# First attention with its rows of values in six visits per group, its lead-in and the middle stage's end reordered

## The reference

```python
x = L0_attn_x                              # (4, 1024, 128), float32
x = _layernorm(x + _L0_attn_ref(x, ...))   # 16 heads of 8
x = _layernorm(x + _L0_ffn_ref(x, ...))    # 8 experts, top 1, hidden 512
x = _layernorm(x + _L1_attn_ref(x, ...))   # 16 heads of 64
x = _layernorm(x + _L1_ffn_ref(x, ...))    # gated, hidden 512
```

```python
Q = proj(Wq, bq); K = proj(Wk, bk); V = proj(Wv, bv)
scores = einsum('bhid,bhjd->bhij', Q, K) / sqrt(hd)
decay = where(causal, 0.0, -abs(delta) ** ALPHA)      # delta = i - j, causal: delta < 0
scores = where(causal, -inf, scores) + decay
attn = softmax(scores, axis=-1)
return einsum('bhij,bhjd->bhid', attn, V) ... @ Wo.T + bo
```

## Time and profile before

| | us |
|---|---|
| three runs | 2277.38, 2282.85, 2283.62 |
| median | 2282.85 |
| the profiled execution | 2285.02 |
| its span, first to last instruction | 2283.2 |
| mean granted clock of PE | 0.951 |

### The profile page before, as it was taken

How to read it: one execution, slowest core, us unless ns; L and a number is a source line. 1 busy time by engine, 2 the same in 40 slices (tenths; PEclk the granted TensorE clock), 3 DMA queues, 4 the chain that set the end, 5 groups by cost and what they waited for, 6 DMA issues and landing times.

```text
span 2283.2 us, 34398 instructions
## 1 busy us (share of the span) xinstructions
PE 2072.3 (91%) x11728; PEld 1169.3 (51%) x11728; DVE 1513.8 (66%) x3409; ACT 1210.0 (53%) x1923; POOL 779.2 (34%) x480
## 2 busy tenths in 40 slices
PE   5899999998487999877999999999999999999998
PEld 2333333334476555544555555555555555655644
DVE  3877777774732778865888878888887875333311
ACT  2366666667343678853656555555565553223232
POOL 5000000000601111003777777777777773000000
PEclk7899999999588999986999999999999999999999
DMA  5233333111265579656666666666666667543300
GB/s 177 95 125 128 120 120 127 57 51 62 98 186 145 172 231 293 200 169 141 170 166 170 165 152 152 150 159 169 163 169 152 164 158 209 135 103 84 88 5 9
DMA packets 230189, 319.11 MB, mean 140 GB/s; under 512 B 22316, under 2 KB 152668, under 8 KB 229608
## 3 DMA queue, kind: packets, MB, share of 16 engines
q1 hardware_dynamic: 214712, 289.04, 46.2%
q0 software_dynamic: 7664, 24.39, 3.0%
q10 hardware_dynamic: 7640, 3.48, 0.5%
HBM read 176.91 MB, written 105.84 MB: 124 GB/s over the span
## 4 chain that ended last, share of the span: by engine, by line
PE 28%; DVE 16%; issue 8%; SPq 1%; DMA 1%; ACT 0%; DVEq 0%
PE ps L1252 10%; DVE a1mx L968 4%; PE ps L916 4%; DVE a1KB L982 3%; DVE a1mx L972 3%; PE ps L900 3%; DVE a1QB L982 3%; PE ps L870 2%; PE ps L901 2%; PE ps L1203 2%; DVE a1mx L965 2%; PE ps L1263 1%; PE ps L1240 1%; PE ps L1241 1%; DVE ps L965 1%
## 5 line engine op out<-in xcount | busy, mean ns | idle before, releaser
L1088 POOL TENSOR_TENSOR a1sum<-a1sum,a1prob 128x1024 f32<-128x1024 f32 (+3 forms) x256 | 489.0, 1910 | 64.9 <-ACT a1prob L1025 33.5
L1025 ACT ACTIVATE a1prob<-ps 128x512 f32<-128x512 f32 (+2 forms) x640 | 326.0, 562 | 252.7 <-PE ps L903 238.4
L468 DVE TENSOR_REDUCE a0grid<-ps 128x8 f32<-128x1024 f32 x288 | 346.7, 1221 | 118.9 <-PE ps L344 64.9
L569 ACT ACTIVATE a0prob<-ps 128x1024 f32<-128x1024 f32 x288 | 292.9, 1025 | 170.2 <-PE ps L370 91.3
L965 DVE CUSTOM_DVE_ANT_0 ps<-ps,c_mask_ij 128x128 f32<-128x128 f32 x496 | 262.7, 551 | 97.2 <-issue 95.5
L900 PE MATMUL ps<-a1QA,a1KA 69*128 69x512 f32 (+3 forms) x768 | 285.7, 379 | 5.8 <-PEq L33 3.4
L916 PE MATMUL ps<-a1prob,a1V 128*64 128x512 f32 (+3 forms) x1536 | 277.9, 505 | 0.0
L870 PE MATMUL ps<-a1KA,a1QA 68*128 68x128 f32 x744 | 241.7, 391 | 28.7 <-DVE a1mx L968 16.4
L901 PE MATMUL ps<-a1QB,a1KB 128*128 128x512 f32 (+3 forms) x768 | 264.4, 352 | 0.0
L916 PEld LDWEIGHTS ps<-a1prob,a1V 128*64 128x64 f32 x1536 | 104.4, 140 | 171.1 <-issue 144.2
L1085 POOL TENSOR_TENSOR a1sum<-a1prob 128x768 f32<-128x768 f32 x64 | 156.8, 2450 | 82.0 <-ACT a1prob L1025 79.9
(11 more groups left out here) (268 smaller groups left out, 3227.5 us busy)
## 6 DMA issues: line engine op xcount, KB each, us to landing
a1FK<-s_k SPq DMA_DIRECT2D x128, 256.0 KB, 5.3
a1FQ<-s_q SPq DMA_DIRECT2D x128, 256.0 KB, 5.8
s_xs<-c_zero POOLq DMA_DIRECT2D x19, 1024.0 KB, 9.0
s_q<-mqkT SPq DMA_DIRECT2D x32, 512.0 KB, 3.0
s_k<-mqkT SPq DMA_DIRECT2D x32, 512.0 KB, 3.0
s_v<-mv SPq DMA_DIRECT2D x32, 512.0 KB, 3.9
a1V<-s_v SPq DMA_DIRECT2D x32, 512.0 KB, 4.4
a1KA<-a1KB SPq DMA_DIRECT2D x64, 256.0 KB
```

What stands on the lines that cost most here:

```text
L468: dve.tensor_reduce(grid[g % 2][:, :, a:b + 1:b - a], banks(("max", k)), axis=AX.X, op=ALU.max).then_inc(s1_free, 1)
L569: act.activation(prob[:, :, a:b + 1:b - a, :], banks(("exp", q)), ACT.Exp).then_inc(p_full, 1)
L1025: act.activation(weights_of(g, u)[:, group[0]:group[-1] + 1, off:BANK], both(e, u, group), ACT.Exp).then_inc(weighed, 1)
L1088: pool.tensor_tensor(t[:, :, off:BANK], t[:, :, off:BANK], weights_of(g, u)[:, :, off:BANK], ALU.add).then_inc(summed, 1)
```

## The change

1. `after` gives the rows in six visits: rows 9, 10, 11 of the group before at unit 2, then 0 and 1 at 6, 2 and 3 at 8, 4 and 5 at 11, 6 and 7 at 14, 8 at 17.
2. Lead-in: three sets of high and low buffers; 13 products ahead instead of 17; PE waits only for drains in banks that the ring uses; SP stores chunk 2 before the loads of K and BQ of group 0, and chunk 4 before the first loads of group 1; ACT issues BK of group 0 after 8 products.
3. End of the middle stage: 12 maxima, the last gate jobs, 12 maxima, turn; ACT splits pair 1 there, and then sends the row of pair 0. `QB1`, `KB1` move into the buffers of the first pair (16 KB more), and the small tiles of the routing move before the assertion on its end.
4. Second attention: SP issues the copies of pair 1 ahead of its slopes and V; DVE lowers pair 1 at units 0 to 3 of group 0; ACT's splits of pair 2 stand behind units 0, 3, 4, 5, as in the other groups.

```diff
@@ -69,8 +69,7 @@
-    after = {1: ((9,), ()), 2: ((10,), ()), 3: ((11,), ()), 5: ((), (0,)), 6: ((), (1,)), 7: ((), (2,)), 8: ((), (3,)),
-             10: ((), (4,)), 11: ((), (5,)), 13: ((), (6,)), 15: ((), (7,)), 17: ((), (8,))}
+    after = {2: ((9, 10, 11), ()), 6: ((), (0, 1)), 8: ((), (2, 3)), 11: ((), (4, 5)), 14: ((), (6, 7)), 17: ((), (8,))}
...
@@ -93,7 +92,7 @@
-    EARLY, NPROD, COL = 17, len(products), dim + 1
+    PARTS3, EARLY, NPROD, COL = 3, 13, len(products), dim + 1
...
@@ -133,7 +132,7 @@
         product, xT_full, high_full, low_full, v_full = sem("product"), sem("xT_full"), sem("high_full"), sem("low_full"), sem("v_full")
-        stored = [sem("stored0"), sem("stored1")]
+        stored = [sem(f"stored{r}") for r in range(PARTS3)]
...
@@ -147,13 +146,21 @@
+        def batch_stored(engine, b):
+
+            for c in range(b * seq // CHUNK, (b + 1) * seq // CHUNK):
+                engine.wait_ge(stored[c % PARTS3], 16 * 4 * (c // PARTS3 + 1))
+
+            batch_stored(engine, g // per)
+            if g > 0:
+                batch_stored(engine, g // per)
...
@@ -171,9 +178,6 @@
-            if h == 0:
-                for r in range(2):
-                    engine.wait_ge(stored[r], 16 * 4 * (b + 1))
...
@@ -190,7 +194,7 @@
-                    nc.sync.dma_start(scr[name][r, :, c * CHUNK:(c + 1) * CHUNK], part[c % 2][:, n, :].bitcast(F32)).then_inc(stored[c % 2], 16)
+                    nc.sync.dma_start(scr[name][r, :, c * CHUNK:(c + 1) * CHUNK], part[c % PARTS3][:, n, :].bitcast(F32)).then_inc(stored[c % PARTS3], 16)
...
@@ -202,12 +206,14 @@
             store(1)
+            batch_stored(sp, 0)
             still(sp, Q[0], "q0", 0, loaded1[0])
-            sp.wait_ge(cleared, 1)
-            load_second(sp, 0)
             for c in range(2, chunks):
                 store(c)
-                if c == 3:
+                if c == 2:
+                    sp.wait_ge(cleared, 1)
+                    load_second(sp, 0)
+                if c == 4:
                     sp.wait_ge(cleared, 2)
...
@@ -418,8 +424,9 @@
                 project(n)
-            for n in range(8, EARLY - 3):
-                drained(n)
+            for n in range(8, EARLY - 1):
+                if n % 8 < 2 * RING:
+                    drained(n)
             pe.wait_ge(const["c_cast"], 4)
...
@@ -508,7 +515,7 @@
                     dve.wait_ge(high_full, 2 * c + i + 1)
-                    dve.scalar_tensor_tensor(low[c % 2][:, i, :], product_bank(n), (bq, bk)[i][:, 0:1], high[c % 2][:, i, :].bitcast(F32),
+                    dve.scalar_tensor_tensor(low[c % PARTS3][:, i, :], product_bank(n), (bq, bk)[i][:, 0:1], high[c % PARTS3][:, i, :].bitcast(F32),
                                              ALU.add, ALU.subtract).then_inc(low_full, 1)
...
@@ -561,8 +568,8 @@
-                    for r in range(2):
-                        act.wait_ge(stored[r], 16 * 4 * chunks // 2)
+                    for r in range(PARTS3):
+                        act.wait_ge(stored[r], 16 * 4 * len(range(r, chunks, PARTS3)))
...
@@ -587,9 +594,9 @@
-                if c > 1:
-                    act.wait_ge(stored[c % 2], 16 * 4 * (c // 2))
-                act.activation(high[c % 2][:, i, :], product_bank(n), ACT.Identity, bias=(bq, bk)[i][:, 0:1]).then_inc(high_full, 1)
+                if c >= PARTS3:
+                    act.wait_ge(stored[c % PARTS3], 16 * 4 * (c // PARTS3))
+                act.activation(high[c % PARTS3][:, i, :], product_bank(n), ACT.Identity, bias=(bq, bk)[i][:, 0:1]).then_inc(high_full, 1)
...
@@ -602,11 +609,12 @@
             cast_constants()
-            for n in range(6, EARLY - 1):
+            for n in range(6, 8):
                 drain(n)
             act.wait_ge(cleared_first, 1)
+            batch_stored(act, 0)
             moving(act, BK[0], "k0", 0, loaded1[0])
-            for n in range(EARLY - 1, NPROD):
+            for n in range(8, NPROD):
                 drain(n)
...
@@ -725,8 +734,8 @@
-        QA, KA, QB, KB = ([first] + [own(f"{n}{b}", [P, 2, S], F32R) for b in range(1, NB)]
-                          for first, n in ((pair0.QA, "QA"), (pair0.KA, "KA"), (pair0.QB, "QB"), (pair0.KB, "KB")))
+        QA, KA = ([first] + [own(f"{n}{b}", [P, 2, S], F32R) for b in range(1, NB)] for first, n in ((pair0.QA, "QA"), (pair0.KA, "KA")))
+        QB, KB = ([first, second, own(f"{n}2", [P, 2, S], F32R)] for first, second, n in ((pair0.QB, pair0.QB1, "QB"), (pair0.KB, pair0.KB1, "KB")))
         FQ, FK = pair0.FQ, pair0.FK
...
@@ -816,9 +825,9 @@
-            load_e(1)
+            load_e(1)
...
@@ -984,8 +993,8 @@
                 for u in range(NU):
-                    if g == 0 and 2 <= u < 6:
-                        lower(1, u - 2)
+                    if g == 0 and u < 4:
+                        lower(1, u)
                     at_units = (2, 6, 10, 11) if g > 0 else (6, 7, 10, 11)
...
@@ -1049,12 +1058,8 @@
                     exponentials(g, u)
-                    if g == 0 and u < 2:
-                        split(1, 2 * u)
-                        split(1, 2 * u + 1)
-                    at_units = (0, 3, 4, 5) if g > 0 else (4, 5, 6, 7)
-                    if g + 2 < G and u in at_units:
-                        split(g + 2, at_units.index(u))
+                    if g + 2 < G and u in (0, 3, 4, 5):
+                        split(g + 2, (0, 3, 4, 5).index(u))
                     if u == TILES - 1:
...
@@ -1964,9 +1969,9 @@
                 here.append((("xT", "gate")[n % 12 // 11], n // 12 + 1, 0))
-            if n == LAST:
-                here += [("max", k, 0) for k in range(NM)] + [("turn", 0, 0)]
+            here += [("max", k, 0) for k in range(NM // 2)] if n == LAST else []
             here += [("aug", c, 0) for c in turn_gates.get(n, ())]
+            here += [("max", k, 0) for k in range(NM // 2, NM)] + [("turn", 0, 0)] if n == LAST else []
             after_item[n] = here
...
@@ -2237,10 +2242,11 @@
-            def first_maxima():
+            def first_maxima(some):
                 mx, mx2 = pair0.mx, pair0.mx2
-                for k, (head, t, j0, j1) in enumerate(max_rows):
+                for k in some:
+                    head, t, j0, j1 = max_rows[k]
                     w, bank = j1 - j0, ps[:, 6 + at["max", k, 0] % 2, :]
...
@@ -2249,6 +2255,9 @@
                         dve.tensor_reduce(mx2[:, 0, head, t - IT // 2:t - IT // 2 + 1], bank[:, 0:w], axis=AX.X, op=ALU.max).then_inc(pair0.max_done, 1)
+            def first_row():
+
+                mx, mx2 = pair0.mx, pair0.mx2
                 dve.wait_ge(pair0.max_done, NM)
...
@@ -2274,10 +2283,12 @@
                 if n == LAST:
-                    first_maxima()
+                    first_maxima(range(NM // 2))
                 for late in (2, 3):
                         gates_b(event_of[EVENTS[n - late][0]])
+            first_maxima(range(NM // 2, NM))
+            first_row()
...
@@ -2381,11 +2392,15 @@
                     split(split_at.index(n))
-                if n == LAST:
-                    act.wait_ge(pair0.max_done, NM + 1)
-                    act.dma_start(pair0.QA[ROW:ROW + 1, :, :].bitcast(F32), pair0.neg[:, 0, :].bitcast(F32)).then_inc(pair0.row_in, 16)
                 for c in turn_gates.get(n, ()):
                     keep_aug(c)
+            act.wait_ge(pair0.loaded_f[1], 16 * 8)
+            for k in range(4):
+                which, head = k % 2, k // 2
+                buf, wide = ((pair0.FK[1], pair0.KB1), (pair0.FQ[1], pair0.QB1))[which]
+                act.activation(wide[:, head, :], buf[:, head, :], ACT.Copy).then_inc(pair0.rounded, 1)
+            act.wait_ge(pair0.max_done, NM + 1)
+            act.dma_start(pair0.QA[ROW:ROW + 1, :, :].bitcast(F32), pair0.neg[:, 0, :].bitcast(F32)).then_inc(pair0.row_in, 16)
```

More of the change, by code:

```diff
@@ L118, in attention0 @@
         xT = [over(f"xT{r}", [P, CHUNK]) for r in range(2)]
-        high, low = ([over(f"{n}{r}", [P, 2, CHUNK], F32R) for r in range(2)] for n in ("high", "low"))
+        high, low = ([over(f"{n}{r}", [P, 2, CHUNK], F32R) for r in range(PARTS3)] for n in ("high", "low"))
         rest = {n: over(n, [P, w * seq]) for n, w in (("a0q", 1), ("a0k", 1), ("a0bq", PAIR), ("a0bk", PAIR))}
@@ L645, in __init__ @@
         self.neg, self.spare = own("neg", [2 * IT, 2, P], F32R), own("spare", [P, 3])
+        self.QB1, self.KB1 = own("QB1", [P, 2, S], F32R), own("KB1", [P, 2, S], F32R)
         sem = lambda n: nc.alloc_semaphore(f"a1_{n}")
@@ L1429, in middle @@
         ye = [own(f"ye{r}", [P, P]) for r in range(RB)]
+        sort = own("sort", [P, 32 + experts * experts + 2 * NT])
+        more, ntile, tri = own("more", [P, experts, 32]), own("ntile", [P, experts]), own("tri", [P, experts, experts])
+        cum, ended, te, st = own("cum", [P, experts]), own("ended", [P, NT, experts]), own("te", [P, NT]), own("startt", [P, NT])
+        started, rowf = own("started", [P, NT, experts]), own("rowf", [P, NT])
+        info = own("info", [P, 2, NT], I32)
```

(5 more changed lines are left out.)

## The result

The changed kernel takes 2294.35 us (median of five runs, 2293.52 to 2300.74) against 2282.85: 1.0064 of the kernel before by the means of the runs, 95% interval 1.0049 to 1.0080, so 11 to 18 us slower (11.5 by the medians). Forecast was +10, to 2292.8. The profiled execution has a span of 2291.9 us against 2283.2.

The account below looks back on a forecast made before the run. PE, 91% busy, was taken as the bound in units with rows, DVE's reductions in units without. Terms +18 - 10 + 2 = +10 on the profiled 2285.0, less 2.2 for the median, gave 2292.8 us; range 2276 to 2305.

Parts of the forecast that it names:

- Part 1: First attention, rows in six visits: PE's saving falls where DVE sets the end; +18 us, bounds +11 and +27.
- The term per group: First attention: six visits lengthen each group of 18 units by 1.3 us, charged over 14.7 groups as +19.1.
- the sum: First attention: unit times, each the larger of 1.22 and 0.67 plus its rows, 25.1 before, 27.2 after: +2.1 per group.
- the replay: First attention: following every unit in program order with measured durations; 29.8 us per group before, 31.1 after.
- The upper bound: Part 1, +27 us: a visit's second row pays its exit as now, making a group 31.7 us, +1.9.
- Part 2: Lead-in: reordered loads and stores bring the first maxima and first exponential earlier; -10 us, bounds -4 and -14.
- Stores 6 and 7: Lead-in: they stand behind group 1's second loads and land near 80, when the first exponential wants them; no size given.
- Another sign: Lead-in: after the change ACT no longer waits for a store; before, it waited until 50.74 with 25.65 idle.
- the Trainium skill's rule (37): Lead-in: slowest dimension fixes a transfer's DMA engines, so loads share two; first maxima at 37 instead of 35, part gives -8.
- Part 3: End of the middle stage: gate jobs between the two twelves of maxima, so scores start at 1031.5 instead of 1032.26; -0.7 us.
- Part 4: Second attention's group 0: ACT's first split of pair 2 holds up exponentials behind it; group ends 2 to 3 us later.
- I take 1048.5: Second attention's group 0: assumed landing of pair 2's last load, 1053.43 before, as it is issued some 6.5 us earlier.

Follow-up runs that it names:

- halved reductions: DVE's first-attention reductions over 64 instead of 128 columns, otherwise the kernel before: 2256.00 us with its twelve visits, 2247.71 with the six-visit table, one run each.
- eleven visits: The kernel before with a table that spreads the rows so that fewest short units stand alone: 2266.43 us, 0.9920 of the kernel before.

## Why the prediction was right, and where by luck

Sign and size held (+10 against +11.5 by the medians, +11 to +18 by the interval), but the touched stages give +16.1, and terms erred both ways.

- **Part 1, +18 forecast, +12.7 in the profiled execution** (+14.3 and -1.5), inside the bounds. The mechanism as stated, PE's saving lost to DVE in the short units, is what the timeline shows, down to "over 4 us" of waits (4.08). The term per group was 1.3, measured 0.85. The visits themselves are not the excess: the sum had 1.88 us for two rows of 512 and 1.43 for 384, 256 and 128 (2.55 and 2.1 less the unit's 0.67), the trace has 1.86 and 1.43. Which step of the replay made a group 31.1 where 30.6 was measured is not shown. The halved reductions narrow the mechanism: DVE is the first to pace, not the only one. And PE's saving, 1.3 to 2.3 in the prediction, was 0.85 to 1.4.
- The upper bound took the Trainium skill's rule on row groups ("TensorE: Matmul & The Clock Gate", Part 3: a weight load runs under a matmul in flight only where their row groups differ) to the letter. But rows in succession pay no exit, 1.86 us for two of 512 where twice 0.99 would be 1.98. The measurement decides against that use of the rule.
- **Part 2, -10 forecast, -2.7 measured**, outside the bounds of -4 and -14. The failed step is the last: "Stores 6 and 7 stand behind the second loads of group 1 and land near 80, just when the first exponential wants them." I saw the meeting and gave it no price. The maxima were negated 8.9 us earlier, as forecast; then the row's two DMAs took 8.8 us from issue to landing, 2.5 before. Another sign held: ACT waits for no store in the lead-in any more. (The high part that waited until 50.74 in the earlier trace rows was that of chunk 4, not of chunk 3; no term hung on it.) First maxima came at 36.9, as by the Trainium skill's rule (37), not 35; that rule deserved the main sum, and its consequence for small transfers behind the loads should have been followed.
- **Part 3, -0.7 forecast, -0.75 measured**, in every kernel with this part (25.6 to 25.7 us against 26.5).
- **Part 4, +2.7 forecast within "parts 3 and 4: +2", +6.8 measured**, +6.1 for both parts, at their bound of +6. The mechanism held, an idle of ACT behind unit 0's exponentials. The step that failed is "I take 1048.5" for the last load: measured from the first scores, 17.0 us was assumed (1031.5 to 1048.5) and 20.9 came. I moved the landing by 4.9 us for an issue 6.5 us earlier (3.7 came), though the engines' share was full there (1.07 and 1.12 now, and already 1.08 from 1044 to 1054 us in the kernel before); bytes ahead had to be counted, not issues.
- Net: part 1 was 5 too dear, part 2 7 too cheap, part 4 4 too cheap. That the total came close is luck: these offset, and three unchanged stages happened to be 7.4 us shorter in the profiled execution. The range, 2276 to 2305, was what deserved trust.

## What to carry to other kernels

Fusing short pieces of work to save switches costs more than it saves where the engines that share a small ring with PE then set the pace in the pieces left bare; replay the order with measured durations and search over placements instead, since that found 1.25 us per group where fusing lost 0.85. Before reordering queues around a late DMA, look how many DMA engines the transfers ahead of it use: a share of 0.23 while everybody waited was a sign of few engines, and splitting the loads was worth 12 us where the reordering was worth 3. Where the DMA share is at its full, count bytes ahead rather than issue times, and never let an in-order engine take a step that needs the last of these bytes ahead of steps that don't.

## What was unexpected of the hardware

A DMA spread over all engines is as late as its slowest part: the row, two DMAs of 8 KB, took 8.8 us while the engines were 0.23 busy, and 28 of its 32 parts had landed after 2.5.

The granted clock of PE fell for single short stretches in the first attention. In each of the five profiled kernels with six visits and whole reductions one or two groups after the first took 1.3 to 1.5 us longer (six groups in all), none in the six with twelve or eleven visits. The clock fell at the same place of the group each time, within 0.3 us of the end of PE's wait for an exponential, and the visit of rows 0 and 1 behind it took 2.7 to 2.9 us instead of 1.64. In the changed kernel:

```profile
249.00:250.00 1.00, 0.83 (x6) 0.19 (x2) 0.95 (x2) 0.86 (x1) 0.00 (x0) 1.00 0.21 74
250.00:251.00 1.00, 0.78 (x4) 0.58 (x4) 0.60 (x1) 1.00 (x2) 0.00 (x0) 0.59 0.21 82
251.00:252.00 1.00, 1.00 (x8) 0.20 (x8) 0.95 (x1) 0.58 (x2) 0.00 (x0) 0.50 0.28 98
252.00:253.00 1.00, 1.00 (x8) 0.20 (x4) 0.28 (x1) 0.52 (x1) 0.00 (x0) 0.50 0.19 70
```

The timeline there, and the same visit in a group at full clock (313.66):

```profile
250.22 0.80 PE L350 MATMUL ps<-a0BK,a0Q 51*128 51x512 f32 x2 [0.34 <-ACT a0prob L576]
...
251.38 2.78 PE L397 MATMUL ps<-a0prob,a0V 128*32 128x512 f32 x16
...
313.66 1.71 PE L397 MATMUL ps<-a0prob,a0V 128*32 128x512 f32 x16
```

The other groups have the same waits at this place and no fall, so the waits alone do not explain it.

With halved reductions it was far more. Two stretches, twelve visits first, then six:

```profile
300.00:400.00 100.00, 92.63 (x760) 39.30 (x758) 44.44 (x77) 61.32 (x65) 3.56 (x5) 0.90 0.31 117
```

```profile
300.00:400.00 100.00, 90.86 (x818) 42.24 (x816) 48.43 (x86) 65.92 (x70) 3.56 (x5) 0.98 0.32 117
```

With twelve visits, where PE shows no wait at full clock, several groups took 29 to 30.8 us instead of 26.1; with six, at most 28.8 instead of 27.25. Of the 8.3 us between the two kernels 3.4 lie here (417 against 420 us for the 15 groups), 1.5 in the last group, and the rest in stages whose code is the same. From 440 us on both were at 1.00 again, with PE as busy as before. What makes the clock fall there stays open.
